# Leaving out the spare TensorE products that fill its waits in a fused two-layer network on one core

## The chip, the cores and the metric

The kernel runs on one core of one Trainium2 chip. The metric is the device time of one execution in microseconds (us); lower is better. A core has TensorE (PE, with its weight loads PEld), VectorE (DVE), ScalarE (ACT), GpSimd (POOL) and SyncE (SP), each working through its own instructions in order and waiting on semaphores for the others.

## What is computed

Two layers are run over x of 4 batches x 512 tokens x 256 features, in float32. Cut to what matters:

```python
x = x + attn(layernorm(x))      # q, k, v by one product; softmax over one score per head
x = x + ffn2(layernorm(x))      # top-1 of 2 experts, FF = 1024, silu(g) * u
x = x + ssm(layernorm(x))       # selective scan, state 8: h = dA * h + dBu; y = sum(h * C) + x * D
x = x + moe(layernorm(x))       # top-6 of 64 experts, F = 176, capacity 64, plus a shared expert
```

## The kernel before

The work is cut by batch (b = 0 to 3, 512 tokens, J = 4 tiles of 128) and by stage. A stage name such as `ssm_sum.2.5` is name, batch, part. The string `plan` (L375) lists all stages in one order written out by hand. `run` (L433) walks this list for each engine, and an engine runs its own piece of a stage if it has one. So one list fixes the order on every engine, and a piece that must wait holds up everything behind it on its engine.

The first part works through attention (`attn_*`), routing (`route_*`) and the two-expert layer (`ffn*`) of all batches. The middle interleaves `ffn*`, the scan (`ssm*`) and the gates of the second expert layer (`gates_in`, `gates`, `places`, `rounds`). Behind the list, `run_pairs` (L445) goes through 32 pairs of experts, one after the other, and the sums at the end follow.

The stages that the prediction speaks of:

- `attn_in` is a layer norm on DVE; `attn_turn` (L673) has PE transpose the normed tiles into `turn_ps` and ACT copy them out; `attn_qkv` (L678, product in L684) is the q, k, v product of one tile, and ACT copies it to `xf` (L914); `attn_score`, `attn_add` and `route_gate` are DVE's, with one exponential each on ACT for `attn_score` and `route_gate`.
- `route_slots` needs two tiny PE products (L693, L694), then DVE (from L1173) works out the rows, and POOL scatters the tokens to memory. `ffn_in` loads them back and transposes them. `ffn` (L705, products in L712) and `ffn_h` (transposes of DVE's result, L652) follow.
- `gates_in` is a norm on DVE (L1101 its last part) with PE transposes (L652) and ACT copies; `gates` is a PE product of 16 records (L780) and DVE's softmax (from L1338); `places` is DVE's top-6 (to L1375), a PE transpose and an ACT copy; `rounds` is DVE's repeated maximum (L1387); `tables` is DVE's (L1415 to L1428, the last two after a PE transpose and an ACT copy), and POOL's gathers of token rows start when it is done.
- `shared_mm` (L794), `shared` (DVE, L1255 and L1260) and `shared_out` (PE, L812) are the shared expert. The first pair of experts starts with `turn_rows(0)` (PE transposes of the gathered rows, L832), then PE waits for `gu_used` (DVE has used the last `shared_mm` product, L874), then comes `gate_up1(0)` (L841).

`awake` (L665) is PE's alone. It multiplies the identity with zeros, twice, 256 columns wide, into `ssm_ps`. Nothing reads that result; the next real product into this bank starts it anew. In batch 0 it waits for POOL's constants, in batch 3 for ACT's last copy out of `ssm_ps`. The list holds 39 of these stages: 16 for batch 0 ahead of and among the attention stages, 23 for batch 3 between `ssm_out.3` and the end of the list.

Each float32 product shows in the trace as two records, so one `awake` stage is four records.

Of the kernel before, what the change touches and what calls it, by code (L numbers as in the profile page):

```python
# [119 lines left out]
def build(nc, x, wq_t, bq, wkv_t, bkv, gate0, wg0_t, wu0_t, wd0_t, wx_t, wdt_t, b_dt, a_log, d_par,  # L120
          gate1_t, wgu1, wd1, shg_t, shu_t, shd_t, out):
    with ExitStack() as ctx:
# [132 lines left out]
        def carve(n):  # L255
# [125 lines left out]
            route_slots.1 ffn.0.0 ffn.0.1 ffn_h.0.0 attn_score.2 awake.0.15 ffn.0.2 ffn_h.0.1 ffn.0.3 attn_turn.3
            attn_add.2 attn_qkv.3.0 ffn_load.1 attn_qkv.3.1 ffn_down.0.0 route_gate.2 ffn_h.0.2 ffn.0.4 ffn_h.0.3
            ffn.0.5 attn_qkv.3.2 attn_qkv.3.3 route_slots.2 ffn_down.0.1 attn_score.3 ffn_h.0.4 attn_add.3 ffn.0.6
            ffn_h.0.5 ffn.0.7 ffn_down.0.2 ffn_h.0.6 route_gate.3 ffn.0.8 ffn_h.0.7 route_slots.3 ffn.0.9
            ffn_down.0.3 ffn_h.0.8 ffn_h.0.9 ffn_down.0.4 ffn_out.0 ffn_in.1 ffn.1.0 ssm_norm.0 ffn.1.1 ffn_h.1.0
            ffn.1.2 ssm_in.0 ssm_proj.0 ffn_h.1.1 ssm_exp.0 ssm_delta.0 ffn.1.3 ffn_down.1.0 ssm.0.0 ffn_h.1.2
            ssm_a.0.0 ffn.1.4 ffn_h.1.3 ffn.1.5 ffn_down.1.1 ssm.0.1 ssm_a.0.1 ssm_sum.0.0 ffn_h.1.4 ssm_a.0.2
            ssm_a.0.3 ssm_a.0.4 ssm.0.2 ffn.1.6 ffn_h.1.5 ssm_sum.0.1 ffn.1.7 ffn_down.1.2 ssm_a.0.5 ssm_sum.0.2
            ssm.0.3 ssm.0.4 ssm.0.5 ssm_a.0.6 ffn_h.1.6 move_sum.0.0 ffn.1.8 ffn_h.1.7 ssm_a.0.7 ffn_load.2 ffn.1.9
# [1126 lines left out]
```

## Time and profile before

| | |
|---|---|
| median of 3 runs | 695.05 us (693.71 to 695.93) |
| the profiled execution: its own time | 695.07 us |
| its span, first to last instruction | 693.3 us |
| mean granted TensorE clock | 0.934 of full |
| busy: PE, DVE, ACT, POOL | 589.8, 514.0, 192.2, 106.4 us |

Times in the trace are us from the span's start. "Granted clock" is the TensorE clock that the throttle allowed in a stretch, as a share of 2.4 GHz; it is at one of two levels, 1.00 (2.4 GHz) or 0.50 (1.2 GHz), and a value between them is a stretch that had both. Releasers in brackets name what ended an engine's idle time. The records of back-to-back PE products overlap by some tenths of a us in the timeline; the chain shows them end to end.

### The profile page before, as it was taken

Reading aid. Unit: us, or ns where it says so; the run is one execution under the profiler, and the core shown is the slowest. Engines: PE = TensorE matmul, PEld = TensorE weight load, DVE = VectorE, ACT = ScalarE, POOL = GpSimd, SP = SyncE. Lnnn points to the kernel's source line nnn. Section 1 sums busy time; section 2 is a strip of 40 time slices with the busy share of each in tenths; the row PEclk is TensorE's granted clock in tenths of the full one; section 3 lists DMA queues with packets and bytes.
Section 4 is the critical chain, followed back from the end, with each engine's and each line's share of the span. In section 5 each row is a group of like instructions: output and inputs, shape, how many; then the busy total and the mean of one; then the engine's idle time right before and its main releaser. Section 6 shows DMA issues by size and latency. Waiting matters only on the chain.

```text
span 693.3 us, 7285 instructions
## 1 busy us (share of the span) xinstructions
PE 589.8 (85%) x2297; PEld 334.7 (48%) x2297; DVE 514.0 (74%) x1126; ACT 192.2 (28%) x375; POOL 106.4 (15%) x120
## 2 busy tenths in 40 slices
PE   7569999789998859987889958949599799999865
PEld 6444565435555346543455513534287344444454
DVE  7989888068895859999689996899978355555355
ACT  1112231136432344322543305413110223323000
POOL 2022020300002000020000030000000456664200
PEclk9889999899999959999799977979899999999999
DMA  7960000419102291010750014993071299996497
GB/s 278 405 208 25 16 32 0 134 66 352 43 0 69 93 353 51 23 38 1 282 182 24 1 38 154 348 333 129 0 251 38 77 330 367 373 374 240 178 413 296
DMA packets 50036, 114.62 MB, mean 165 GB/s; under 512 B 6096, under 2 KB 32464, under 8 KB 49488
## 3 DMA queue, kind: packets, MB, share of 16 engines
q1 hardware_dynamic: 42064, 94.36, 38.0%
q0 software_dynamic: 5632, 17.70, 7.3%
q10 hardware_dynamic: 2304, 2.10, 0.9%
q8 instruction: 20, 0.33, 0.2%
q14 instruction: 16, 0.13, 0.1%
HBM read 83.99 MB, written 30.15 MB: 165 GB/s over the span
## 4 chain that ended last, share of the span: by engine, by line
PE 50%; DVE 33%; DMA 6%; issue 4%; ACT 3%; SPq 2%; POOL 1%; DVEq 0%; POOLq 0%; ACTq 0%
PE gate_ps L712 7%; DVE scan_area L1315 7%; PE gate_ps L841 6%; PE up_ps L712 6%; PE misc_ps L729 5%; DMA bc<-part_rows 4%; DVE scan_area L1311 3%; DVE scan_area L1318 3%; PE turn_ps L652 3%; PE ssm_ps L671 3%; PE ssm_ps L761 3%; PE ssm_ps L859 3%; PE misc_ps L812 3%; PE misc_ps L859 3%; SPq L563 2%
## 5 line engine op out<-in xcount | busy, mean ns | idle before, releaser
L1315 DVE TENSOR_TENSOR_SCAN scan_area<-scan_area 128x1024 f32<-128x1024 f32 x32 | 73.3, 2292 | 4.4 <-ACT scan_area L999 0.9
L712 PE MATMUL gate_ps<-big,front_area 128*128 x144 | 74.8, 645 | 1.4 <-ACT front_area L899 1.4
L761 PE MATMUL ssm_ps<-scan_area,ident 128*128 128x512 f32 x128 | 63.5, 629 | 12.6 <-DVE scan_area L1318 11.9
L712 PE MATMUL up_ps<-big,front_area 128*128 x144 | 70.1, 610 | 0.0
L729 PE MATMUL misc_ps<-big,front_area 128*128 x288 | 65.6, 381 | 4.2 <-ACT front_area L899 3.8
L729 PEld LDWEIGHTS misc_ps<-big,front_area 128*128 128x128 f32 x288 | 54.3, 190 | 18.3 <-issue 11.7
L935 ACT ACTIVATE sig<-gate_ps 128x512 f32<-128x512 f32 (+1 forms) x48 | 28.5, 595 | 105.2 <-PE up_ps L712 65.9
L671 PE MATMUL ssm_ps<-zeros,ident 128*128 128x256 f32 x156 | 42.1, 427 | 15.9 <-ACT front_area L899 12.9
L999 ACT ACTIVATE scan_area<-scan_area,a_col 128x511 f32<-128x511 f32 x64 | 42.2, 714 | 39.8 <-DVE scan_area L1315 35.8
L610 POOL DMA_INDIRECT front_area<-ysorted_dram,slot_idx x16 | 18.5, 1155 | 188.0 <-DMA ysorted_dram<-front_area 184.4
L712 PEld LDWEIGHTS up_ps<-big,front_area 128*128 128x128 f32 x144 | 29.0, 201 | 37.9 <-issue 37.9
L761 PEld LDWEIGHTS ssm_ps<-scan_area,ident 128*128 128x128 f32 x128 | 24.5, 197 | 44.1 <-issue 25.4
L671 PEld LDWEIGHTS ssm_ps<-zeros,ident 128*128 128x128 f32 x156 | 33.1, 217 | 22.8 <-ACT front_area L899 13.6
L1318 DVE TENSOR_TENSOR scan_area<-scan_area,bc 128x1024 f32<-128x1024 f32 x32 | 39.2, 1225 | 1.1
L1255 DVE SCALAR_TENSOR_TENSOR sig<-sig,gate_ps 128x512 f32<-128x512 f32 (+1 forms) x48 | 32.8, 683 | 9.7 <-ACT sig L935 9.3
L1311 DVE TENSOR_TENSOR scan_area<-scan_area,bc 128x1024 f32<-128x1024 f32 x32 | 39.1, 1223 | 0.5
L899 ACT COPY front_area<-turn_ps 128x512 f32<-128x512 f32 (+1 forms) x56 | 31.1, 575 | 25.2 <-PE turn_ps L652 24.2
L712 PEld LDWEIGHTS gate_ps<-big,front_area 128*128 128x128 f32 x144 | 26.8, 204 | 23.2 <-issue 23.2
L635 POOL DMA_INDIRECT part_rows<-bc,att_s x32 | 31.2, 974 | 37.6 <-DVE bc L1446 36.8
L619 POOL DMA_INDIRECT bc<-table,att_s x32 | 30.9, 965 | 28.8 <-DVE att_s L1428 19.4
L652 PE MATMUL turn_ps<-ident,front_area 128*128 128x128 f32 x188 | 29.2, 288 | 6.3 <-DMA front_area<-sorted_dram 4.1
L652 PEld LDWEIGHTS turn_ps<-ident,front_area 128*128 128x128 f32 x188 | 23.6, 148 | 21.7 <-issue 11.9
(236 smaller groups left out, 904.9 us busy)
## 6 DMA issues: line engine op xcount, KB each, us to landing
bc<-bc_dram SPq DMA_DIRECT2D x4, 4096.0 KB, 13.3
part_rows<-zeros SPq DMA_DIRECT2D x16, 768.0 KB, 15.8
big<-in_wgu SPq DMA_DIRECT2D x15, 704.0 KB
front_area<-in_wgu SPq DMA_DIRECT2D x9, 704.0 KB
big<-part_rows SPq DMA_DIRECT2D x8, 768.0 KB, 9.6
...
```

The costliest lines, as they stand in the source:

```text
L652: mm = pe.transpose(turn_ps[slot][0:width, col:col + rows], src, ident[0:rows, 0:rows])
L671: pe.matmul(ssm_ps[:, 0:D], ident[:], zeros[:, 0:D], start=True, stop=True)
L712: mm = pe.matmul(bank[:], xs_t[:, k, j, :], gu0[:, expert_of[b, j], k, g, half * 512:(half + 1) * 512], start=(k == 0), stop=(k == K - 1))
L729: mm = pe.matmul(misc_ps[:, 0:D], h0_t[:, half, c * P:(c + 1) * P], dn0[:, expert_of[b, j], half * 4 + c, :], start=(half == 0 and c == 0) ...
L761: mm = pe.matmul(ssm_ps[:], ident[:], hs[:, g % HS_RING, n, :], start=False, stop=(g % PER_CHUNK == PER_CHUNK - 1 and n == GROUP - 1))
L841: mm = pe.matmul(gate_ps[p % 2][e * CAP:(e + 1) * CAP, 0:FSH], xg_t[:, p % 2, k, e * CAP:(e + 1) * CAP], gu1[p % RING][:, e * K + k, :], s ...
L859: mm = pe.matmul(y_ps[par][e * CAP:(e + 1) * CAP, 0:D], h1_t[0:rows, par, c, e * CAP:(e + 1) * CAP], dn1[p % RING][c][:, e * D:(e + 1) * D ...
L999: nc.scalar.activation(d_a[:, g % 2, n, 1:L], delta[:, c, 1:L], ACT.Exp, scale=a_col[:, c, n0 + n:n0 + n + 1]).then_inc(da_ready, 1)
L1255: stt(out=s, in0=s, scalar=1.0, in1=gate_ps[slot][0:rows, :], op0=ALU.add, op1=ALU.mult).then_inc(silu_steps, 1)
L1311: tt(buf, sp_z[:, c, :].unsqueeze(1).broadcast_to([P, GROUP, L]), bc[:, n0:n0 + GROUP, :], ALU.mult).then_inc(dbu_ready, 1)
L1315: nc.vector.tensor_tensor_scan(buf.rearrange(flat), d_a[:, g % 2, :, :].rearrange(flat), buf.rearrange(flat), 0.0, ALU.mult, ALU.add).then ...
L1318: tt(buf, buf, bc[:, NS + n0:NS + n0 + GROUP, :], ALU.mult).then_inc(hc_ready, 1)
```

## The change

All 39 `awake` stages are taken out of the list. The function `awake` stays, unused, and all other stages keep their order. Cut to its core:

```diff
-            awake.0.0 awake.0.1 awake.0.2 awake.0.3 awake.0.4 awake.0.5 attn_in.0 attn_turn.0 awake.0.6 awake.0.7
-            attn_in.1 attn_qkv.0.0 attn_qkv.0.1 attn_qkv.0.2 attn_in.2 attn_qkv.0.3 awake.0.8 attn_score.0
...
+            attn_in.0 attn_turn.0 attn_in.1 attn_qkv.0.0 attn_qkv.0.1 attn_qkv.0.2 attn_in.2 attn_qkv.0.3
+            attn_score.0 attn_turn.1 attn_add.0 route_gate.0 attn_qkv.1.0 ffn_load.0 attn_qkv.1.1 attn_qkv.1.2
...
```

Only PE's instructions change; those of the other engines are the same, with the same waits. The text of the change is four lines shorter, so a line of before from L641 on has a number lower by 4 after.

PE at the start, before, from just behind `attn_qkv.0.3` to `attn_qkv.2.1` (`front_area` and `scan_area` hold the normed tiles; `ssm_ps<-zeros` are the `awake` products):

```order
L671 MATMUL ssm_ps<-zeros,ident 128x256 x2
L652 MATMUL turn_ps<-ident,scan_area 128x128 x8
L671 MATMUL ssm_ps<-zeros,ident 128x256 x6
L684 MATMUL turn_ps<-w_qkv,front_area 128x288 x2
L671 MATMUL ssm_ps<-zeros,ident 128x256 x4
L684 MATMUL turn_ps<-w_qkv,front_area 128x288 x4
L693 MATMUL misc_ps<-rt,before_me 128x4
L694 MATMUL misc_ps<-rt,ones 128x4
L684 MATMUL turn_ps<-w_qkv,front_area 128x288 x2
L652 MATMUL turn_ps<-ident,scan_area 128x128 x8
L671 MATMUL ssm_ps<-zeros,ident 128x256 x2
L684 MATMUL turn_ps<-w_qkv,front_area 128x288 x4
```

The same place after:

```order
L648 MATMUL turn_ps<-ident,scan_area 128x128 x8
L680 MATMUL turn_ps<-w_qkv,front_area 128x288 x6
L689 MATMUL misc_ps<-rt,before_me 128x4
L690 MATMUL misc_ps<-rt,ones 128x4
L680 MATMUL turn_ps<-w_qkv,front_area 128x288 x2
L648 MATMUL turn_ps<-ident,scan_area 128x128 x8
L680 MATMUL turn_ps<-w_qkv,front_area 128x288 x4
```

The four groups of spare products are gone. The transposes of batch 1 are followed at once by `attn_qkv.1.0` to `attn_qkv.1.2` (two calls each), and those of batch 2 by `attn_qkv.2.0` and `attn_qkv.2.1`.

PE at the end of the list, before, from `ssm_out.3` over `gates_in.3`, `gates.3`, `places.3` and `shared_out.2.1` to `shared_mm.3.0`:

```order
L652 MATMUL turn_ps<-ident,back_t 128x128 x8
L671 MATMUL ssm_ps<-zeros,ident 128x256 x16
L652 MATMUL turn_ps<-ident,xf 128x128 x8
L780 MATMUL misc_ps<-w_g,gate_t 128x64 x8
L671 MATMUL ssm_ps<-zeros,ident 128x256 x16
L652 MATMUL turn_ps<-ident,marked 128x128 x2
L812 MATMUL misc_ps<-w_shd,hsh_t 128x256 x6
L671 MATMUL ssm_ps<-zeros,ident 128x256 x8
L794 MATMUL gate_ps<-gate_t,w_sh 128x512 x2
```

The same place after:

```order
L648 MATMUL turn_ps<-ident,back_t 128x128 x8
L648 MATMUL turn_ps<-ident,xf 128x128 x8
L776 MATMUL misc_ps<-w_g,gate_t 128x64 x8
L648 MATMUL turn_ps<-ident,marked 128x128 x2
L808 MATMUL misc_ps<-w_shd,hsh_t 128x256 x6
L790 MATMUL gate_ps<-gate_t,w_sh 128x512 x2
```

Here 40 spare products in three groups are gone, 16 ahead of `gates_in.3`, 16 ahead of `places.3`, 8 ahead of `shared_mm.3.0`.

PE a little later, before, from the second half of `shared_mm.3.1` over `tables` and `shared_mm.3.2` to the first pair of experts:

```order
L794 MATMUL up_ps<-gate_t,w_sh 128x512 x2
L671 MATMUL ssm_ps<-zeros,ident 128x256 x2
L652 MATMUL turn_ps<-ident,work 128x64
L794 MATMUL gate_ps<-gate_t,w_sh 96x512 x2
L794 MATMUL up_ps<-gate_t,w_sh 96x512 x2
L671 MATMUL ssm_ps<-zeros,ident 128x256 x4
L832 MATMUL turn_ps<-ident,bc 128x128 x2
L841 MATMUL gate_ps<-big,bc 64x352 x4
```

The same place after:

```order
L790 MATMUL up_ps<-gate_t,w_sh 128x512 x2
L648 MATMUL turn_ps<-ident,work 128x64
L790 MATMUL gate_ps<-gate_t,w_sh 96x512 x2
L790 MATMUL up_ps<-gate_t,w_sh 96x512 x2
L828 MATMUL turn_ps<-ident,bc 128x128 x2
L837 MATMUL gate_ps<-big,bc 64x352 x4
```

Two spare products ahead of the transpose of `tables` and four ahead of `turn_rows(0)` (L832) are gone.

## Rows read from the trace of the kernel before

**Rows 1.** The page: engines, chain by engine, the group of the spare products.

```profile
PE 589.8 (85%) x2297; PEld 334.7 (48%) x2297; DVE 514.0 (74%) x1126; ACT 192.2 (28%) x375; POOL 106.4 (15%) x120
...
PE 50%; DVE 33%; DMA 6%; issue 4%; ACT 3%; SPq 2%; POOL 1%; DVEq 0%; POOLq 0%; ACTq 0%
...
L671 PE MATMUL ssm_ps<-zeros,ident 128*128 128x256 f32 x156 | 42.1, 427 | 15.9 <-ACT front_area L899 12.9
```

**Rows 2.** Chain that ended last, 500 to 562 us: start, length, what.

```profile
507.38 6.91 PE ssm_ps L671 x32
...
517.99 6.96 PE ssm_ps L671 x32
...
527.77 3.46 PE ssm_ps L671 x16
...
538.09 0.86 PE ssm_ps L671 x4
...
543.13 1.73 PE ssm_ps L671 x8
...
545.63 1.40 PE gate_ps L841 x8
```

**Rows 3.** DVE's timeline, 512 to 546 us: start, length, what.

```profile
513.23 1.38 DVE L1101 TENSOR_SCALAR xf<-x_res,ln_mv,ln_w 128x256 f32<-128x256 f32 x4
518.03 0.42 DVE L1338 TENSOR_REDUCE sc_s<-misc_ps 128x4 f32<-128x256 f32 x1 [3.42 <-PE misc_ps L780]
...
523.75 0.43 DVE L1375 TENSOR_TENSOR marked<-att_s,sc 128x256 f32<-128x256 f32 x1
...
537.27 0.35 DVE L1419 SCALAR_TENSOR_TENSOR work<-work 64x64 f32<-64x64 f32 x2
...
544.51 0.75 DVE L1260 SCALAR_TENSOR_TENSOR hsh_t<-sig,up_ps 96x256 f32<-96x256 f32 x2
```

**Rows 4.** DVE's timeline, 39 to 66 us.

```profile
39.62 0.17 DVE L1173 COPY rt<-misc_ps 128x8 f32<-128x8 f32 x1 [1.54 <-PE misc_ps L694]
...
41.17 1.36 DVE L1119 TENSOR_TENSOR xf<-xf,b_qkv 128x1152 f32<-128x1152 f32 x1 [0.32 <-ACTq L917]
...
64.36 0.69 DVE L1260 SCALAR_TENSOR_TENSOR front_area<-sig,up_ps 128x512 f32<-128x512 f32 x1
```

**Rows 5.** PE's timeline, 27 to 67 us.

```profile
27.54 5.22 PE L671 MATMUL ssm_ps<-zeros,ident 128*128 128x256 f32 x12 [7.19 <-ACT front_area L899]
...
38.01 1.24 PE L684 MATMUL turn_ps<-w_qkv,front_area 128*128 128x288 f32 x4 [1.58 <-ACT xf L914]
...
48.73 4.05 PE L684 MATMUL turn_ps<-w_qkv,front_area 128*128 128x288 f32 x8
53.17 1.09 PE L652 MATMUL turn_ps<-ident,front_area 128*128 128x128 f32 x8 [0.40 <-DMA front_area<-sorted_dram]
...
63.05 1.88 PE L712 MATMUL up_ps<-big,front_area 128*128 x4
...
65.60 1.03 PE L671 MATMUL ssm_ps<-zeros,ident 128*128 128x256 f32 x4
```

**Rows 6.** Busy time by stretch: PE, PEld, DVE, ACT, POOL; then granted clock, DMA.

```profile
24.00:27.00 3.00, 0.00 (x0) 0.00 (x0) 2.54 (x6) 0.73 (x3) 0.00 (x0) 0.76 1.03 411
30.00:33.00 3.00, 3.00 (x10) 2.39 (x9) 2.75 (x14) 0.00 (x0) 0.00 (x0) 0.61 1.02 406
...
460.00:463.00 3.00, 3.00 (x9) 2.41 (x9) 2.97 (x2) 1.10 (x2) 0.00 (x0) 0.59 1.04 335
```

**Rows 7.** PE's timeline: the gate stages and shared_out of batches 0, 2 and 3.

```profile
241.48 1.97 PE L652 MATMUL turn_ps<-ident,xf 128*128 128x128 f32 x8
244.12 3.68 PE L780 MATMUL misc_ps<-w_g,gate_t 128*128 128x64 f32 x16 [0.68 <-ACT gate_t L899]
...
458.94 4.49 PE L812 MATMUL misc_ps<-w_shd,hsh_t 128*128 128x256 f32 x12
...
516.00 2.00 PE L780 MATMUL misc_ps<-w_g,gate_t 128*128 128x64 f32 x16 [0.67 <-ACT gate_t L899]
```

More of the change, by code:

```diff
@@ L381, in build @@
[L381 to L389, printed above, removed]
-            ssm_sum.0.3 ssm_sum.0.4 ffn_down.1.3 ssm_sum.0.5 ffn_h.1.8 ffn_h.1.9 ssm.0.6 ffn_down.1.4 ssm.0.7
@@ L411, in build @@
-            awake.3.21 awake.3.22 awake.3.23 gates_in.3 gates.3 awake.3.24 awake.3.25 awake.3.26 awake.3.27
-            awake.3.28 awake.3.29 awake.3.30 awake.3.31 places.3 rounds.3.0 rounds.3.1 shared_out.2.1 awake.3.32
-            awake.3.33 rounds.3.2 awake.3.34 awake.3.35 shared_mm.3.0 shared_mm.3.1 awake.3.36 shared.3.0 tables.3
-            shared.3.1 shared.3.2 shared_mm.3.2 awake.3.37 awake.3.38"""
+            attn_in.0 attn_turn.0 attn_in.1 attn_qkv.0.0 attn_qkv.0.1 attn_qkv.0.2 attn_in.2 attn_qkv.0.3
@@ new lines, in build @@
+            ffn_down.1.2 ssm_a.0.5 ssm_sum.0.2 ssm.0.3 ssm.0.4 ssm.0.5 ssm_a.0.6 ffn_h.1.6 move_sum.0.0 ffn.1.8
+            ffn_h.1.7 ssm_a.0.7 ffn_load.2 ffn.1.9 ssm_sum.0.3 ssm_sum.0.4 ffn_down.1.3 ssm_sum.0.5 ffn_h.1.8
+            ffn_h.1.9 ssm.0.6 ffn_down.1.4 ssm.0.7 ffn_out.1 ffn_in.2 ssm_sum.0.6 ssm_sum.0.7 ffn_load.3 move_sum.0.1
+            ssm_out.0 ffn.2.0 ssm_norm.1 ffn.2.1 ffn_h.2.0 ffn.2.2 ssm_in.1 ssm_proj.1 gates_in.0 gates.0 ssm_exp.1
+            places.0 ffn_h.2.1 ssm_delta.1 ssm_a.1.0 rounds.0.0 ffn.2.3 ssm.1.0 ffn_down.2.0 ffn_h.2.2 ffn.2.4
@@ new lines, in build @@
+            move_sum.2.1 shared.0.0 ssm_sum.2.7 ssm_out.2 ssm_norm.3 shared_mm.0.2 shared.0.1 ssm_in.3 ssm_proj.3
+            gates_in.2 shared.0.2 shared_out.0.0 ssm_exp.3 weights_ahead.3 ssm_delta.3 shared_out.0.1 shared_mm.1.0
+            shared.1.0 ssm.3.0 ssm_a.3.0 ssm_a.3.1 shared_mm.1.1 shared.1.1 shared.1.2 shared_mm.1.2 ssm_a.3.2
+            gates.2 places.2 ssm_a.3.3 ssm_a.3.4 ssm.3.1 shared_out.1.0 rounds.2.0 weights_more.3 ssm.3.2
+            shared_out.1.1 ssm_sum.3.0 ssm.3.3 shared_mm.2.0 shared_mm.2.1 shared.2.0 ssm.3.4 shared.2.1 ssm_sum.3.1
@@ L416, in stage_of @@
+            ssm_a.3.5 ssm_a.3.6 shared_mm.2.2 ssm_sum.3.2 ssm_sum.3.3 ssm_sum.3.4 ssm.3.5 shared.2.2 move_sum.3.0
+            ssm_sum.3.5 ssm_sum.3.6 ssm_a.3.7 ssm.3.6 ssm_sum.3.7 ssm.3.7 rounds.2.1 rounds.2.2 shared_out.2.0
+            move_sum.3.1 ssm_out.3 gates_in.3 gates.3 places.3 rounds.3.0 rounds.3.1 shared_out.2.1 rounds.3.2
+            shared_mm.3.0 shared_mm.3.1 shared.3.0 tables.3 shared.3.1 shared.3.2 shared_mm.3.2"""
         def stage_of(name, batch, part="0"):
```

42 lines of the change are left out of this document (19 added, 23 removed).

## The prediction

> **What bounds the kernel now.** I read the page first, for the shares. The trap is in its first line: PE is busy 85% of the span, and the spare products alone are 42.1 us of that [rows 1]. The chain of waits says something else. It runs over PE for half of the span and over DVE for a third [rows 1], so the two take turns, and a product that PE does while DVE sets the pace costs nothing. Then the chain in order of time, at the end of the list: the spare products stand on it as 6.91, 6.96, 3.46, 0.86 and 1.73 us, together 18.9 us [rows 2]. They stand there because each runs up to the moment at which the next real stage can start, or a little past it. What would have been waited for without them must be read from DVE's timeline [rows 3, 4]. Last the granted clock by stretch, and products of one shape at both clocks [rows 5 to 7], since a product that nobody reads can still have an effect on the next one.
>
> What these show of the clock: PE had nothing to do for 7.19 us before 27.54 [rows 5], and in that time the granted clock fell (0.76 in 24 to 27, where it did nothing at all) [rows 6]. The spare products that followed began at 1.2 GHz: 12 records took 5.22 us [rows 5], where 32 take 6.91 at the full clock [rows 2]. In 30 to 33 the mean is 0.61, so 2.3 of these 3 us were still at 1.2 GHz and the clock came back at about 32.3, after 4.8 us of steady work. In 460 to 463 the mean is 0.59 [rows 6]: back at about 462.5, 3.5 us after the group that began at 458.94 [rows 7]. A product at 1.2 GHz takes 1.6 to 1.85 times as long: the gate stage 3.68 us against 2.00 [rows 7], eight records of the q, k, v product 4.05, so 2.02 for four, against 1.24 [rows 5].
>
> **The start (16 stages).** Up to 27 us DVE goes from norm to norm and PE is ahead of it; I cost the first nine stages at nothing. The cover is that DVE takes up the first scores only after its third norm, when PE and ACT have long had the operand ready; were it gone, each product there would be late by its own price at the lower clock.
>
> Then, after ACT's copies at 27.5, qkv.1.0 and qkv.1.1 run at once, at 1.2 GHz, 2.02 us each, and end at 31.6. In place of spare products PE has nothing until 38.01, when ACT frees a buffer [rows 5]. That is 6.4 us, close to the 7.19 that let the clock fall. So qkv.1.2 starts at 38.01 as before but at 1.2 GHz: +0.8. The two tiny products of the routing add 0 to 0.5 (no row at the lower clock; I take 0.25). DVE is waiting for them: 1.54 us at 39.62 [rows 4], so the routing of batch 0 is 1.05 late, and with it POOL's scatter and the load for ffn_in.0. qkv.1.3 adds another 0.8, and DVE waits for it at 41.17 (0.32 now) [rows 4]: DVE is 1.9 late from there. The spare stage ahead of qkv.2.0 goes, four records at the lower clock (5.22 / 12 x 4 = 1.7); the operand of qkv.2.0 is now 1.9 later, so it starts at 48.7 to 48.9, all but the same, and at 1.2 GHz as before (4.05 for eight records) [rows 5].
>
> The two lines meet at the first expert products. PE's (ffn.0.1) ended at 63.05 + 1.88 = 64.93 and now ends at 66.0. DVE's result (64.36 + 0.69 = 65.05 [rows 4]) comes at 66.95, and PE's transposes wait for that. Behind them stood one more spare stage, 0.87 us from start to start (65.60 [rows 5] to the next product). PE goes on 1.9 - 0.87 = **1.0 us late**, and here PE is busy without gaps, so this stays.
>
> What is open is when the clock comes back. PE's steady work now begins at 48.7 and stops at 52.8 to wait for the load of ffn_in.0, until about 53.17 + 1.05 = 54.2 [rows 5]. That is 4.1 us of work, between the two recoveries read above (3.5 and 4.8). If the clock is back, nothing more is lost. If not, the transposes and q, k, v products that follow cost about 2.7 more (1.8 for eight records of q, k, v by the two prices above, 0.9 for ten transposes at nearly twice their time), of which 1.0 is hidden, since DVE's result is 1.0 behind PE's. So the start costs 1.0 to 2.7; I take **1.5**, nearer to the low end, because a clock that comes back by 56 costs nothing extra.
>
> **The end of the list (23 stages).** Before, PE filled the 6.9 us until gates_in.3. Now it has nothing from 507.4 until DVE's first two normed tiles, at 513.23 + half of 1.38 = 513.9 [rows 3]. 6.5 us idle: the clock falls, as above. The transposes and gate products at the lower clock are those of batch 0: 241.48 to 244.12 + 3.68 = 247.80, so 6.3 us [rows 7], and end at 520.2 against 516.00 + 2.00 = 518.0 [rows 7]. That is **+2.2**. DVE waits for them (3.42 us already [rows 3]), so it all counts.
>
> DVE's gates and places take 6.15 us either way, to 523.75 + 0.43 = 524.18 before [rows 3] and 526.4 now. Before, the third group of spare products kept PE until 517.99 + 6.96 = 524.95 [rows 2]: 0.8 given back. The transpose at the lower clock costs 0.3 more. DVE's maxima start later by 2.2 - 0.8 + 0.3: **+1.7**.
>
> DVE has the slots for tables at 537.27 + 0.35 = 537.6 [rows 3], but PE is in shared_mm and spare products until 538.09 + 0.86 = 538.95 [rows 2]. Now DVE is ready at 539.3. Is PE? Its shared_out.2.1 starts at 527.0 and takes 4.5 as in batch 2 [rows 7], to 531.5. Without the next spare products (3.46 [rows 2]) shared_mm.3.0 and 3.1 follow, 6.9 us, to 538.4. It is free 0.9 us ahead of DVE. So tables is late by 539.3 - 538.95 = 0.35, and another 1.35 us are given back. shared_mm.3.2 starts with it and DVE is done with it at 544.51 + 0.75 = 545.26 [rows 3], now 545.6. The first pair began at 545.63 behind the last spare products (to 544.86) [rows 2]; its rows had landed by then, and their gathers are 0.35 late too. It begins at 545.9 to 546.1: the end of the list costs **0.3 to 0.5**. I take 0.3. From there PE's steady loop over 32 pairs is the same.
>
> Between the two places nothing changes but by the shift: each cold spell there falls somewhat otherwise, either way.
>
> **Sum.** The profiled execution took 695.07, 1.8 more than its span, and is the same as the median, 695.05. 695.07 + 1.5 + 0.3 = **696.9**. With the ends 1.0 to 2.7 and 0.3 to 0.5, and half a us for each of the shifted cold spells' sides, this forecast's own range is 695.4 to 698.8.
>
> The Trainium skill ("TensorE: Matmul & The Clock Gate", HAM oscillation) prices this another way: what a throttled stretch costs is its length times one half. For single products the trace agrees (3.68 against 2.00). Applied to every added throttled stretch, about 18 us at the end and 10 at the start by my working, it would give an estimate of 14 us and 709; here most of such a stretch is waiting for DVE, which no clock shortens.
>
> **Rivals.**
>
> *The clock stays up.* Then only what the spare products delayed is left: 0.87 at 65.6, and at the end 0.2 of waiting at 514, 0.8 at 524.95 and 1.35 before tables, which DVE's chain hands on in full. 695.07 - 0.9 - 2.3 = 691.9. It needs 6.4 us without work at the full clock; 7.19 us [rows 5] did not pass without a fall. Decided at 514. 8%.
>
> *All is hidden.* DVE's lateness of 1.9 meets the 0.87 given back and some wait behind it that I did not see, and the end comes out at zero: 695.1. For it: the chain changes engine often. Against: both lines are late by 1.0 at 66 us and the stretch behind has no gap. 12%.
>
> *The clock comes back late,* slower. The place is 54 to 62 us: if the clock stays at 1.2 GHz through the first expert products, 7.8 us of PE's time hold half of the work, 3.9 lost, 1.0 of it hidden by DVE: start 3.9. At the end the same length from 527.0 brings shared_mm.3.1 to 540.4, 1.1 behind DVE's slots: end 1.2 to 1.4. 700.2. It decides from the point at which the clock is not back by 56 us. For it: the work is broken by a wait at 52.8 to 54.2. Against: both recoveries above. 18%.
>
> *The change takes effect as waits and nothing else* (the chain's 18.9 us vanish, 676): nothing in DVE's timeline gets shorter with it. Under 1%.
>
> **The numbers.** Forecast 62%, the rivals 8, 12 and 18%. A change of under 0.3% (2.1 us) can't be told from none here. The forecast's range is cut by 697.15 a little above its middle: 35% same, 27% slower. Same: 35 and 12, 47%; slower: 27 and 17, 44%; faster 9%. The range 693.8 to 700.3 leaves out the fast rival and the worst of the slow one.
>
> **What would show it.** The granted clock at 0.50 from 33 or 36 to beyond 42, and around 514 to 530. The q, k, v record group at 38 at about 2.0 us. DVE's wait before the first exponential of batch 1 (L1119 before) about 2.2 us. The gate products at the end at 3.7, DVE's maxima 1.7 later than the shift from the start; tables' transpose with no PE work ahead of it. If the first pair starts more than 3 us late against 545.63, the start or the recovery was mis-sized; if it starts earlier, the clock did not fall.

## The result, and the profile after

| | before | after |
|---|---|---|
| median, in turn on one chip | 694.98 us (691.05 to 696.43, 20 runs) | 697.87 us (695.15 to 702.68, 20 runs) |
| the profiled execution, its span | 695.07, 693.3 us | 696.94, 695.2 us |
| mean granted TensorE clock | 0.934 | 0.909 |

The ratio is 1.0047, 95% interval 1.0029 to 1.0064: the kernel without spare products is slower, by 2.0 to 4.4 us, about 3.3. Each ratio here and below is worked out from all the single executions of both kernels, so it need not be the quotient of the two medians (1.0042 here). The prediction had 696.9 as the time, +1.9 us. The profiled execution of after happens to show just that; that is luck, and the median shows more.

The page of after, engines and chain by engine; they answer to [rows 1]:

```profile
PE 562.8 (81%) x2141; PEld 310.7 (45%) x2141; DVE 513.8 (74%) x1126; ACT 192.7 (28%) x375; POOL 105.2 (15%) x120
...
PE 42%; DVE 39%; DMA 7%; issue 4%; ACT 4%; SPq 2%; POOL 1%; DVEq 0%; POOLq 0%; ACTq 0%
```

PE lost 156 instructions and 42.1 us of spare work, but its busy time fell by only 27.0 us: the other 15 are real products that now take longer. The chain has 8 points less of PE and 6 points more of DVE: what stood there as spare products stands there now as waiting for DVE.

Busy time by stretch, after; columns as in [rows 6], the granted clock is the third number from the end:

```profile
24.00:27.00 3.00, 0.00 (x0) 0.00 (x0) 2.54 (x6) 0.62 (x2) 0.00 (x0) 0.50 1.02 411
...
36.00:39.00 3.00, 0.88 (x2) 0.74 (x3) 1.86 (x12) 0.79 (x3) 0.00 (x0) 0.50 1.08 312
39.00:42.00 3.00, 3.00 (x9) 2.31 (x9) 0.80 (x6) 0.40 (x1) 0.00 (x0) 0.50 1.06 332
...
51.00:54.00 3.00, 2.13 (x5) 1.07 (x4) 2.86 (x11) 0.80 (x2) 0.00 (x0) 0.70 0.66 207
54.00:57.00 3.00, 2.17 (x13) 1.59 (x14) 2.69 (x12) 1.45 (x3) 0.00 (x0) 1.00 0.00 0
...
514.00:534.00 20.00, 9.61 (x35) 8.36 (x36) 11.47 (x49) 1.96 (x4) 0.40 (x1) 0.50 0.46 156
534.00:536.00 2.00, 2.00 (x8) 1.30 (x7) 1.90 (x6) 0.00 (x0) 0.00 (x0) 0.98 0.00 0
```

The clock is at its low level from 36 to 42, back before 54, and at the low level for all 20 us from 514 to 534, where before had the full clock (1.00, its row stands in experiment 3). That is the forecast's picture.

PE's timeline at the start, after; it answers to [rows 5]:

```profile
38.12 2.29 PE L680 MATMUL turn_ps<-w_qkv,front_area 128*128 128x288 f32 x4 [6.26 <-ACT xf L910]
40.20 0.43 PE L689 MATMUL misc_ps<-rt,before_me 128*128 128x4 f32 x2
...
56.36 2.21 PE L680 MATMUL turn_ps<-w_qkv,front_area 128*128 128x288 f32 x8 [0.46 <-ACT front_area L895]
...
67.35 0.66 PE L648 MATMUL turn_ps<-ident,front_area 128*128 128x128 f32 x4 [1.22 <-DVE front_area L1256]
67.84 1.45 PE L708 MATMUL gate_ps<-big,front_area 128*128 x3
```

The third tile of batch 1 starts at 38.12 as before and takes until 40.20, at 1.2 GHz. By 56.36 the clock is up: eight records take 2.21 us. PE then waits 1.22 us for DVE at 67.35, and `ffn.0.2` starts at 67.84 against 66.47.

DVE's timeline at both ends, after; it answers to [rows 3, 4]:

```profile
41.10 0.17 DVE L1169 COPY rt<-misc_ps 128x8 f32<-128x8 f32 x1 [2.90 <-PE misc_ps L690]
...
43.45 1.36 DVE L1115 TENSOR_TENSOR xf<-xf,b_qkv 128x1152 f32<-128x1152 f32 x1 [1.12 <-ACTq L913]
...
516.55 1.38 DVE L1097 TENSOR_SCALAR xf<-x_res,ln_mv,ln_w 128x256 f32<-128x256 f32 x4
...
523.72 0.42 DVE L1334 TENSOR_REDUCE sc_s<-misc_ps 128x4 f32<-128x256 f32 x1 [5.78 <-PE misc_ps L776]
...
531.18 0.49 DVE L1383 MAX8 keep<-work 128x8 f32<-128x320 f32 x1 [1.33 <-ACT work L895]
...
542.77 0.35 DVE L1415 SCALAR_TENSOR_TENSOR work<-work 64x64 f32<-64x64 f32 x2
...
548.81 0.75 DVE L1256 SCALAR_TENSOR_TENSOR hsh_t<-sig,up_ps 96x256 f32<-96x256 f32 x2
```

Against [rows 4], DVE has the routing's sums 1.48 us late (41.10) and starts on the second batch's q, k, v 2.28 late (43.45). The last norm is 3.32 late (516.55 against 513.23 in [rows 3]), the softmax behind it 5.69, the slots for `tables` (L1415, L1419 before) 5.50, the last `shared` 4.30. So from the norm on the end adds 2.4 at the softmax, 2.2 at the slots and 1.0 at the last `shared`.

PE's timeline at the end, after; it answers to [rows 2, 7]:

```profile
517.39 1.94 PE L648 MATMUL turn_ps<-ident,xf 128*128 128x128 f32 x8 [6.66 <-DVE xf L1097]
520.01 3.67 PE L776 MATMUL misc_ps<-w_g,gate_t 128*128 128x64 f32 x16 [0.68 <-ACT gate_t L895]
530.00 0.66 PE L648 MATMUL turn_ps<-ident,marked 128*128 128x128 f32 x2 [6.33 <-DVE marked L1371]
...
543.18 0.28 PE L648 MATMUL turn_ps<-ident,work 64*128 64x64 f32 x1 [1.31 <-DVE work L1415]
...
549.61 1.40 PE L837 MATMUL gate_ps<-big,bc 128*64 128x352 f32 x8 [1.54 <-DVE hsh_t L1256]
```

PE waits for DVE in front of each step but the gate products, which wait 0.68 for ACT's copy and take 3.67. The first pair starts at 549.61, 3.98 late, of which 3.32 came with the last norm: the end costs 0.66 here. Of the 3.32, `ffn.0.2` had only 1.37; the rest came in the long stretch between, in which no stage was changed. Yet the whole span is only 1.9 longer. Of the other 2.1, 1.8 are in a place that the prediction took for the same in both: in before, PE stops once more at the third pair (below, experiment 9).

### The profile page after: what moved, and what is told of

It is laid out like the page before. It is cut to its first block, busy times and chain, and to the rows that moved or that the text cites. A ratio compares the mean times of both kernels' runs of the same rounds, so it can differ in the third digit from the quotient of the medians.

```text
span 695.2 us, 6972 instructions
## 1 busy us (share of the span) xinstructions
PE 562.8 (81%) x2141; PEld 310.7 (45%) x2141; DVE 513.8 (74%) x1126; ACT 192.7 (28%) x375; POOL 105.2 (15%) x120
## 4 chain that ended last, share of the span: by engine, by line
PE 42%; DVE 39%; DMA 7%; issue 4%; ACT 4%; SPq 2%; POOL 1%; DVEq 0%; POOLq 0%; ACTq 0%
DVE scan_area L1311 7%; PE gate_ps L837 6%; PE gate_ps L708 6%; PE up_ps L708 5%; PE misc_ps L725 4%; DMA bc<-part_rows 4%; DVE scan_area L1307 3%; DVE scan_area L1314 3%; PE turn_ps L648 3%; PE ssm_ps L855 3%; PE misc_ps L855 3%; DVE work L1385 2%; DVE sig L1251 2%; DVE keep L1383 2%; PE misc_ps L808 2%
## 5 line engine op out<-in xcount | busy, mean ns | idle before, releaser
L708 PE MATMUL gate_ps<-big,front_area 128*128 x144 | 72.7, 630 | 1.4 <-ACT front_area L895 1.4
L995 ACT ACTIVATE scan_area<-scan_area,a_col 128x511 f32<-128x511 f32 x64 | 42.3, 714 | 41.0 <-DVE scan_area L1311 36.2
L648 PE MATMUL turn_ps<-ident,front_area 128*128 128x128 f32 x188 | 30.6, 297 | 20.2 <-DVE front_area L1097 8.9
L680 PE MATMUL turn_ps<-w_qkv,front_area 128*128 128x288 f32 x64 | 25.0, 551 | 22.1 <-ACT front_area L895 15.9
L611 POOL COPY xf<-sc 128x256 f32<-128x256 f32 x4 | 2.1, 527 | 190.9 <-DVE sc L1343 190.9
## 6 DMA issues: line engine op xcount, KB each, us to landing
front_area<-in_wgu SPq DMA_DIRECT2D x9, 704.0 KB, 14.6
```

The costliest lines, as they stand in the source:

```text
L648: mm = pe.transpose(turn_ps[slot][0:width, col:col + rows], src, ident[0:rows, 0:rows])
L708: mm = pe.matmul(bank[:], xs_t[:, k, j, :], gu0[:, expert_of[b, j], k, g, half * 512:(half + 1) * 512], start=(k == 0), stop=(k == K - 1))
L995: nc.scalar.activation(d_a[:, g % 2, n, 1:L], delta[:, c, 1:L], ACT.Exp, scale=a_col[:, c, n0 + n:n0 + n + 1]).then_inc(da_ready, 1)
```

## The experiments

The theory: the spare products act through the clock alone, and the start makes most of the loss. Its rivals: what they earn lies at the end (the gate products at 3.67 instead of 2.00); or it isn't the clock at all, but the order and the number of the instructions. Where an expectation has theories with letters, these are its own. All kernels are cut from the kernel before; each median and ratio is against executions of before on the same chip in the same session (12 of the kernel, or 10, and 33 to 35 of before). Before's own median was 695.1 to 697.7 from chip to chip, so the ratio counts. The diffs are cut to the stages that change.

**Experiment 1: only the 16 stages of batch 0 out.**

```diff
-            awake.0.0 awake.0.1 awake.0.2 awake.0.3 awake.0.4 awake.0.5 attn_in.0 attn_turn.0 awake.0.6 awake.0.7
...
-            route_slots.1 ffn.0.0 ffn.0.1 ffn_h.0.0 attn_score.2 awake.0.15 ffn.0.2 ffn_h.0.1 ffn.0.3 attn_turn.3
```

> Only the 16 spare stages of batch 0 are out. If the loss comes from the lower clock at the start, as predicted: +1.0 to +1.9 us against before (about 0.2%), DVE's wait for the second q, k, v copy 2 us longer, the first expert products behind ffn_h.0.0 1.0 to 1.4 us late. If the loss is made at the end of the list: 0 here. If removing the stages is neutral there and only moves code, 0.

Measured: 698.28 against 695.5 us, ratio 1.0043 (1.0024 to 1.0062), 3.0 us slower, where 1.0 to 1.9 was expected. The start alone costs as much as the whole change. In its profile the clock comes back late at the products that the prediction had left open (PE's timeline; eight records that take 2.21 us in the first profile of after):

```profile
57.06 3.90 PE L683 MATMUL turn_ps<-w_qkv,front_area 128*128 128x288 f32 x8 [0.46 <-ACT front_area L898]
```

**Experiment 2: only the 23 stages of batch 3 out.**

```diff
-            shared_out.2.0 move_sum.3.1 ssm_out.3 awake.3.16 awake.3.17 awake.3.18 awake.3.19 awake.3.20 awake.3.21
...
-            shared.3.1 shared.3.2 shared_mm.3.2 awake.3.37 awake.3.38"""
+            shared.3.1 shared.3.2 shared_mm.3.2"""
```

> Only the 23 spare stages of batch 3 are out. The theory of the prediction: the gate products at the end start at 1.2 GHz, +2.2 at DVE's softmax, of which 0.3 to 0.7 are left at the first pair of experts; time +0.3 to +1.0 us. Rival: the end makes most of the measured 3.3 us, +2 us or more, because more of the 2.2 us stays than I counted. The two runs together should give the whole, 3.3 us, if the places are independent.

Measured: 693.65 against 695.5 us, ratio 0.997 (0.9955 to 0.9986): 2.1 us faster. Leaving out the products at the end is a gain, where I had put +0.3. So they earn nothing at the end, taken as a whole, as far as this run goes; experiment 8 finds no gain in leaving them out. Its profile is the forecast's for the end, with the clock low behind it (PE's timeline, this kernel):

```profile
513.21 1.94 PE L650 MATMUL turn_ps<-ident,xf 128*128 128x128 f32 x8 [8.08 <-DVE xf L1099]
515.82 3.68 PE L778 MATMUL misc_ps<-w_g,gate_t 128*128 128x64 f32 x16 [0.68 <-ACT gate_t L897]
...
539.57 3.56 PE L792 MATMUL gate_ps<-gate_t,w_sh 128*96 128x512 f32 x4 [0.30 <-ACT bc L897]
```

**Experiment 3: all 39 stages stay, each product 8 columns wide.** Same instructions in the same places with the same waits, and little for PE to do in them.

```diff
-                    pe.matmul(ssm_ps[:, 0:D], ident[:], zeros[:, 0:D], start=True, stop=True)
+                    pe.matmul(ssm_ps[:, 0:8], ident[:], zeros[:, 0:8], start=True, stop=True)
```

> All 39 spare stages stay in their places with their waits, but each product is 8 columns wide instead of 256, so PE has the same number of instructions and little work. If what counts is the clock that the work keeps up, the time is that of the changed kernel, +2.5 to +3.5 us, with the clock at 1.2 GHz at 38 and at 516. If what counts is anything that hangs on the instructions being there (their place in the code, PE being awake to its semaphores), the time is that of before, within 1 us.

Measured: 698.71 against 695.5 us, ratio 1.0044 (1.0023 to 1.0064). Busy time by stretch, this kernel:

```profile
27.00:45.00 18.00, 14.93 (x48) 11.66 (x48) 12.63 (x48) 2.38 (x7) 1.38 (x2) 0.52 0.90 320
514.00:534.00 20.00, 17.18 (x76) 16.08 (x76) 11.30 (x44) 1.96 (x4) 0.40 (x1) 0.54 0.32 110
```

and before:

```profile
27.00:45.00 18.00, 12.61 (x48) 9.71 (x48) 15.00 (x49) 2.07 (x6) 2.78 (x2) 0.85 0.91 326
514.00:534.00 20.00, 19.33 (x95) 15.66 (x94) 13.74 (x47) 1.96 (x4) 0.40 (x1) 1.00 0.26 91
```

The records show PE busy for 14.93 of 18 us, and the granted clock is at its low level nearly all the time (0.52; before had 0.85 there). With every instruction and wait in place the loss is the full one. So it isn't the order or the count of instructions but the work that the products give the engine.

**Experiment 4: six of the 39 out,** those that reach past the moment at which real work could start: the one ahead of `ffn.0.2`, the last of the second group at the end, and the last four of the list.

```diff
-attn_score.2 awake.0.15 ffn.0.2
+attn_score.2 ffn.0.2
...
-awake.3.28 awake.3.29 awake.3.30 awake.3.31 places.3
+awake.3.28 awake.3.29 awake.3.30 places.3
...
-awake.3.34 awake.3.35 shared_mm.3.0 shared_mm.3.1 awake.3.36 shared.3.0
+awake.3.34 shared_mm.3.0 shared_mm.3.1 shared.3.0
...
-shared.3.1 shared.3.2 shared_mm.3.2 awake.3.37 awake.3.38"""
+shared.3.1 shared.3.2 shared_mm.3.2"""
```

> 33 of 39 spare stages stay; out are those that the chain shows to delay the next real stage: the one before ffn.0.2, the last one before the transpose of places.3, the last one before shared_mm.3.0 and the one before tables, and the two before the first pair. If waiting for DVE is what the others fill, and the clock stays up without these six: -0.9 at 66 us and -2.1 at the first pair, together -3.0 us against before (0.996). Rival: the clock falls in a gap left by them, or what is given back is lost behind another wait: -1 us or less.

Measured: 694.1 (688.04 to 695.72) against 695.5 us, ratio 0.9966 (0.9943 to 0.9989), 2.4 us faster, near the 3.0 expected; with 0.8 to 4.0 as its interval it all but rules out the rival's 1 or less.

**Experiment 5: the changed kernel again,** with a second profile.

> The changed kernel once more, beside the next three on one chip. The start alone measured +3.0 us and the end alone -2.1 us, which adds up to +0.9, against +3.3 for the whole. If the two parts are independent and the gap is noise: about +1 to +2 us now. If what the end gives is lost when the start is out as well: +3 us again.

Measured: 697.87 against 695.08 us, ratio 1.0046 (1.0022 to 1.0071): the same as the first time. The profile is not the same. PE's timeline at the start, this execution:

```profile
54.30 2.48 PE L648 MATMUL turn_ps<-ident,front_area 128*128 128x128 f32 x10 [0.80 <-DMA front_area<-sorted_dram]
57.25 4.21 PE L680 MATMUL turn_ps<-w_qkv,front_area 128*128 128x288 f32 x8 [0.46 <-ACT front_area L895]
...
69.04 1.88 PE L708 MATMUL gate_ps<-big,front_area 128*128 x4
```

The eight records that took 2.21 us at 56.36 in the first profile take 4.21 here, and `ffn.0.2` starts at 69.04, 2.6 late instead of 1.4. The clock comes back late. The time is the expectation's second case: what the end gives by itself (-2.1) doesn't show when the start is out as well.

**Experiments 6 and 7: only the first nine stages out (`awake.0.0` to `0.8`), and only the next five (`0.9` to `0.13`).**

```diff
-            awake.0.0 awake.0.1 awake.0.2 awake.0.3 awake.0.4 awake.0.5 attn_in.0 attn_turn.0 awake.0.6 awake.0.7
-            attn_in.1 attn_qkv.0.0 attn_qkv.0.1 attn_qkv.0.2 attn_in.2 attn_qkv.0.3 awake.0.8 attn_score.0
+            attn_in.0 attn_turn.0
+            attn_in.1 attn_qkv.0.0 attn_qkv.0.1 attn_qkv.0.2 attn_in.2 attn_qkv.0.3 attn_score.0
```

```diff
-            attn_turn.1 attn_add.0 awake.0.9 awake.0.10 route_gate.0 awake.0.11 attn_qkv.1.0 awake.0.12 ffn_load.0
-            awake.0.13 attn_qkv.1.1 attn_qkv.1.2
+            attn_turn.1 attn_add.0 route_gate.0 attn_qkv.1.0 ffn_load.0
+            attn_qkv.1.1 attn_qkv.1.2
```

> Only awake.0.0 to awake.0.8 are out, those ahead of and among the first batch's attention, up to 19 us. Prediction: 0 (DVE sets the pace there and PE's results have over 2 us in hand, also at 1.2 GHz). Rival: part of the start's 3.0 us comes from here, +1 us or more, because the clock is down when the work at 27 us begins.

> Only awake.0.9 to awake.0.13 are out, the five between 27.5 and 36 us (ten products). If they carry the start's loss by keeping the clock up for attn_qkv.1.2, the routing products and attn_qkv.1.3: DVE 2.0 to 2.7 us late at attn_score.1, and with the stage before ffn.0.2 still there, nothing of it is given back: +2.5 to +3.0 us. Rival: the loss is spread over the sixteen, +1 us or less here.

Measured: 696.48 against 695.08, ratio 1.0026 (1.0001 to 1.005), and 696.82, ratio 1.0029 (1.0011 to 1.0047). The five cost 2.0 us (0.8 to 3.3): less than the 2.5 to 3.0 of the clock theory, more than the rival's 1, and no sharp test between them. The nine cost 1.8, with an interval that all but reaches zero; I had put them at nothing, and the rival had +1 or more. PE's timeline with the nine out:

```profile
8.82 1.94 PE L652 MATMUL turn_ps<-ident,front_area 128*128 128x128 f32 x8 [8.82 <-DVE front_area L1101]
11.44 6.50 PE L684 MATMUL turn_ps<-w_qkv,front_area 128*128 128x288 f32 x16 [0.68 <-ACT front_area L899]
...
57.33 3.81 PE L684 MATMUL turn_ps<-w_qkv,front_area 128*128 128x288 f32 x8 [0.46 <-ACT front_area L899]
```

The first transposes and q, k, v products run in part at 1.2 GHz, which DVE hides for the most part: in this profile the first group behind batch 0's attention starts at 28.25 instead of 27.54 [rows 5], 0.7 us late, and so do the routing's sums (40.34 against 39.62 in [rows 4]). But the clock falls elsewhere too, and eight records at 57.33 take 3.81 us: `ffn.0.2` is 3.1 late. Why that happens here, some 40 us behind the last stage taken out, isn't settled by one execution.

**Experiment 8: the 23 stages at the end and the one ahead of `ffn.0.2` out.**

```diff
-attn_score.2 awake.0.15 ffn.0.2
+attn_score.2 ffn.0.2
...
-            shared.3.1 shared.3.2 shared_mm.3.2 awake.3.37 awake.3.38"""
+            shared.3.1 shared.3.2 shared_mm.3.2"""
```

> Out are the 23 stages of batch 3 and awake.0.15, the one before ffn.0.2; the 15 at the start that come before it stay. Sum of what was measured and read: -2.1 us for the end, -0.9 for the one stage, together -3.0 us against before. Rival: the end's gain was chance or the stage is hidden: -1.5 us or less.

Measured: 694.12 against 695.08 us, ratio 1.0001 (0.9975 to 1.0026). Expected was -3.0; what came is the rival's case, -1.5 or less. It should have been no slower than experiment 2 and is not told from before. The two intervals (0.9955 to 0.9986, 0.9975 to 1.0026) overlap only just, so the gain of experiment 2 isn't confirmed by this one.

**Experiment 9: before again,** as if it were a change.

> The kernel before, unchanged, taken as if it were a change. It says what a comparison of this kind gives when nothing differs, and gives a second profile of before. Theory A (the fall of the clock in before's last part is chance from one execution to the next): the ratio is 1.000 within 0.002, and the 34.2 us from the last norm tile to the first pair's tanh product, seen in the first profile of before, may as well be 37.5 here, with spare products at half clock between 518 and 526 and rounds.3 late. Theory B (the 34.2 us belongs to the kernel with all 39 spare stages, and the 37.5 to those with fewer): 34.2 again. Also: the 2.1 us in which PE issued nothing after the first pair should not be here again.

Measured: ratio 0.9995 (0.9972 to 1.0017). The comparison finds nothing where nothing is. The second profile of before is another picture than the first. Its PE timeline at the end, and its clock:

```profile
504.36 7.07 PE L671 MATMUL ssm_ps<-zeros,ident 128*128 128x256 f32 x32
512.61 1.26 PE L652 MATMUL turn_ps<-ident,xf 128*128 128x128 f32 x8 [1.18 <-issue]
514.54 3.08 PE L780 MATMUL misc_ps<-w_g,gate_t 128*128 128x64 f32 x16 [0.68 <-ACT gate_t L899]
517.41 9.42 PE L671 MATMUL ssm_ps<-zeros,ident 128*128 128x256 f32 x32
526.67 0.38 PE L652 MATMUL turn_ps<-ident,marked 128*128 128x128 f32 x2
...
553.91 1.40 PE L841 MATMUL gate_ps<-big,bc 128*64 128x352 f32 x8 [2.08 <-issue]
```

```profile
517.00:520.00 3.00, 3.00 (x9) 2.54 (x10) 1.76 (x5) 0.42 (x1) 0.00 (x0) 0.50 0.00 0
520.00:523.00 3.00, 3.00 (x11) 2.43 (x9) 2.75 (x18) 0.00 (x0) 0.40 (x1) 0.66 0.50 177
```

The clock falls during the gate products although 7.07 us of spare work stand ahead of them, and then the second group of spare products itself runs at 1.2 GHz: 9.42 us instead of 6.96 [rows 2]. DVE's places were done at 523.80. The real transpose can't start until 526.67, because PE works in order and its queue is full of products that nobody reads. DVE's maxima (L1387) start 15.80 us behind the last norm (511.77), where the first profile of before has 525.69 - 513.23 = 12.46, and after has 14.63. DVE's timeline, this execution:

```profile
523.38 0.42 DVE L1375 TENSOR_TENSOR marked<-att_s,sc 128x256 f32<-128x256 f32 x1
...
527.57 0.49 DVE L1387 MAX8 keep<-work 128x8 f32<-128x320 f32 x1 [3.77 <-ACT work L899]
```

and the first of before:

```profile
525.69 0.49 DVE L1387 MAX8 keep<-work 128x8 f32<-128x320 f32 x1 [1.51 <-ACT work L899]
```

The Trainium skill ("TensorE: Matmul & The Clock Gate", on the HAM clock gate) says that the count of slow products at the start of one and the same kernel differs from run to run. The two profiles of before agree, and show it in the kernel's last part too (6.96 against 9.42 us for the same 32 records).

The wait of 2.08 us at the third pair was there again, which I had expected not to be. In the first profile of before it is this row:

```profile
552.06 1.40 PE L841 MATMUL gate_ps<-big,bc 128*64 128x352 f32 x8 [2.11 <-issue]
```

PE needs two things there: DVE's result of the second pair, which needs ACT's tanh, and ACT's copy of the third pair's turned rows (L1033), which stands behind that tanh in ACT's order. ACT's timeline, the second execution:

```profile
552.03 0.32 ACT L1044 ACTIVATE bc<-gate_ps 128x176 f32<-128x176 f32 x1 [2.33 <-PE gate_ps L841]
553.44 0.37 ACT L1033 COPY bc<-turn_ps 128x256 f32<-128x256 f32 x1 [1.09 <-remote]
```

The products for the tanh start at 549.84 and take 1.40, so they are done at 551.24, and ACT takes them up 0.8 later; in the first profile of before it is 1.5 (550.87 against 549.36). The copy comes another 1.09 later here, and PE starts 0.1 behind its end in both (553.91 against 553.81, 552.06 against 551.96): it is ACT's copy that PE waits for last. From the first to the last of the pairs' tanh products on DVE both executions of before have 95.8 us; the eight of after (twice) and experiments 1, 2, 4, 6, 7 and 8 have 94.0. What holds ACT up isn't shown. It isn't the stages at the end by themselves, since 1, 6 and 7 keep them all. Nor is it a rule of the number of stages: experiment 3 has all 39 and no such stop (its 95.75 us come from a low clock at the first pairs, as the 96.12 of experiment 12), and experiment 11 with 30 stages has one of 2.27 us. So 1.8 us of before's length lie in this loop in both its profiles, and whether the change takes them away or chance does stays open.

**Experiments 10 and 11: the end taken apart.** In both the stage ahead of `ffn.0.2` is out. Experiment 10 keeps of the end only the first group (`awake.3.16` to `3.23`, ahead of `gates_in.3`); experiment 11 keeps all but that group.

```diff
-awake.3.24 awake.3.25 awake.3.26 awake.3.27 awake.3.28 awake.3.29 awake.3.30 awake.3.31 places.3
+places.3
```

```diff
-ssm_out.3 awake.3.16 awake.3.17 awake.3.18 awake.3.19 awake.3.20 awake.3.21 awake.3.22 awake.3.23 gates_in.3
+ssm_out.3 gates_in.3
```

> Of the end only the first group of eight spare stages stays, the one ahead of gates_in.3; all later ones and the one ahead of ffn.0.2 are out. Theory A (at the end, what costs is that spare products stand in the way of real ones, and what they earn is the gate products of gates.3 at the full clock, 2.2 us): the gate products run at 2.0, DVE's softmax is not late, nothing stands ahead of the placed tokens' transpose and of tables, and the time is the least of all: about 1 us below the kernel without any end stage, 692 to 693.5, ratio 0.994 to 0.997. Theory B (the first group alone can't hold the clock through the idle time after it, and DVE's chain decides the rest): as without end stages, 693.5 to 694.5, ratio 0.997 to 0.999. Slower than before would speak against both.

> The opposite: the first group of eight ahead of gates_in.3 and the one stage ahead of ffn.0.2 are out, the other 15 end stages stay. Theory A: the gate products run at 1.2 GHz, 3.7 us, so DVE's softmax is 2.2 late; the spare products behind them begin at 1.2 GHz too and run past the moment at which the placed tokens could be transposed, which adds 1 to 3 us; no gain from the clock left. Worse than before: 696 to 699, ratio 1.002 to 1.006. Theory B (the later groups are harmless, since DVE has slack there): 693.5 to 695, as without end stages.

Measured: experiment 10, 692.96 (689.47 to 696.34) against 697.65 us, ratio **0.9934** (0.9906 to 0.9963), 4.6 us faster than before, Theory A's time or a little better. Experiment 11, 698.77, ratio 1.0008 (0.9986 to 1.0029), between its two theories. PE's timeline of experiment 10:

```profile
513.92 3.22 PE L779 MATMUL misc_ps<-w_g,gate_t 128*128 128x64 f32 x16 [0.68 <-ACT gate_t L898]
523.48 0.66 PE L651 MATMUL turn_ps<-ident,marked 128*128 128x128 f32 x2 [6.33 <-DVE marked L1374]
...
536.65 0.27 PE L651 MATMUL turn_ps<-ident,work 64*128 64x64 f32 x1 [1.03 <-DVE work L1418]
```

and of experiment 11:

```profile
513.51 3.68 PE L780 MATMUL misc_ps<-w_g,gate_t 128*128 128x64 f32 x16 [0.68 <-ACT gate_t L899]
516.98 8.69 PE L671 MATMUL ssm_ps<-zeros,ident 128*128 128x256 f32 x32
525.50 0.38 PE L652 MATMUL turn_ps<-ident,marked 128*128 128x128 f32 x2
```

In 10, PE is idle when DVE comes with the places: the transpose follows at once, and the maxima start 13.51 us behind the norm. In 11 it has to get through 8.69 us first, and they start at 16.35. By the two ratios the difference is 0.74%, 5 us, of which the profiles show 2.84 at the maxima and 4.34 at the first pair (33.74 and 38.08 us behind the norm).

Experiment 8 is the common base of the two: 10 has the first group more than 8 (0.9934 against 1.0001, the intervals apart, on two chips), 11 the 15 later stages more (1.0008 against 1.0001, the same). So the first group is worth having, and the later ones alone show no gain. But it isn't worth it in the way that Theory A had: in the profile of 10 the gate products take 3.22 us, not 2.0, and DVE's softmax comes 1.2 us later behind the norm than in the first profile of before (6.03 against 4.80). That is still less than the 3.67 in the profile of 8, and part of the gain lies further on: `shared_mm.3.2`'s first products take 1.96 us in 10 and 3.56 in 8 and 2.

In the times of experiment 10 the luck of the clock can be seen as well: its four slowest executions (695.4 to 696.3 us) have a mean granted clock of 0.914 to 0.916, the other eight (689.5 to 693.5) 0.928 to 0.933.

**Experiment 12: experiment 4 again.**

> The kernel with 33 spare stages again (out: the one ahead of ffn.0.2, the last of the second end group, and the last four of the list). The first time it stood at 0.9966 of before, with executions of 688.0 to 695.7. Theory A (shorter groups end before the real work can start, so they cost nothing, and the clock's gain stays): again 0.995 to 0.998, with some executions near 688. Theory B (the first result was the luck of that chip): 0.999 to 1.001.

Measured: 695.03 against 697.65 us, ratio 0.9957 (0.9932 to 0.9982). It held, 0.9966 and 0.9957, though no execution came near 688 (the lowest is 691.79). Its profile has 8.56 us for the shorter second group (28 records, at the lower clock), where the first had 6.26: so it too reached past DVE's places when the clock fell. Its interval overlaps that of experiment 10; which of the two is better isn't settled.

Where the 14 profiled executions stood, in us, each read from a row's start (PE L712's third group; DVE L1101, L1387, L1453, with the lines of before):

| kernel | `ffn.0.2` starts | last norm tile | norm to maxima | norm to first tanh product | first to last of these |
|---|---|---|---|---|---|
| before | 66.47 | 513.23 | 12.46 | 34.19 | 95.83 |
| 9, before again | 66.56 | 511.77 | 15.80 | 37.54 | 95.79 |
| after | 67.84 | 516.55 | 14.63 | 34.86 | 93.99 |
| 5, after again | 69.04 | 515.27 | 14.64 | 36.55 | 94.00 |
| 1, start out | 68.54 | 514.81 | 15.79 | 37.52 | 94.01 |
| 6, nine out | 69.59 | 517.53 | 12.46 | 34.19 | 94.00 |
| 7, five out | 69.55 | 514.74 | 15.80 | 37.53 | 94.00 |
| 3, narrow | 68.65 | 515.31 | 14.89 | 36.36 | 95.75 |
| 2, end out | 66.83 | 512.37 | 14.64 | 36.55 | 93.99 |
| 8, end and one out | 67.41 | 512.76 | 14.63 | 36.55 | 93.99 |
| 4, trimmed | 65.74 | 509.25 | 12.66 | 32.88 | 93.99 |
| 12, trimmed again | 67.34 | 513.71 | 14.93 | 35.60 | 96.12 |
| 10, first group kept | 66.16 | 511.15 | 13.51 | 33.74 | 94.67 |
| 11, later groups kept | 65.58 | 510.05 | 16.35 | 38.08 | 99.08 |

The columns from the norm on say it for the end. With all its spare products in place (before, 9, 1, 6, 7) it is 12.5 or 15.8 us long to the maxima, by the luck of the clock: the gate products take 2.00 us in the two short ones and 3.02 to 3.19 in the three long ones. Without them (after, 5, 2, 8) it is 14.6 each time. To the first tanh product the two sorts are alike in the mean, 36.2 and 36.1 us.

The first two columns hold something else: from `ffn.0.2` to the last norm, where no kernel differs from another, it takes 443.5 (experiment 4) to 448.7 us (after), and in before alone 446.8 and 445.2. A single profile can be off by more than the whole effect there.

## Why the prediction was right, and where it wasn't

The mechanism held, in each of its steps: PE's idle time lets the clock fall, DVE waits for the slow products, and the loss is a few us, since most of a slow stretch is waiting that no clock shortens. 697.9 is within the forecast's own range, 695.4 to 698.8. But the chances leaned a little to "within 0.3%" (47 to 44), and it is slower by 0.47%: the terms were too small on balance, and some of them had the wrong place.

- **The start, +1.5 (1.0 to 2.7): too small.** By experiment 1 the whole start costs 3.0 us (1.7 to 4.3). The step that failed was "a clock that comes back by 56 costs nothing extra", taken as the likelier case. In the first profile of after it came back in time, and `ffn.0.2` was 1.4 late. In the second, and in that of experiments 1 and 6, it didn't: 4.21, 3.9 and 3.81 us for eight records that take 2.21. Over the three executions with all 16 stages out (after twice, 1) `ffn.0.2` is 1.3 to 2.5 late, 2.0 in the mean against the two of before (68.5 and 66.5). In experiments 6 and 7 it is 3.1 and 3.0 late, in part since there the 0.87 of the stage ahead of it isn't given back. That was the mechanism of my rival "the clock comes back late", and its condition, low through the first expert products, was asking too much: low through the q, k, v products at 57 is enough. The other step is "between the two places nothing changes but by the shift": at the last norm the three stand 3.1 late in the mean (515.5 against 512.5 for before, 9 and 2), about 1 more than at `ffn.0.2`. With a spread there of 1.5 us in before alone, whether this 1 belongs to the change is open.
- **The size of its steps.** I priced `qkv.1.2` at +0.8, as 2.02 - 1.24; but 1.24 is the time from its first record's start to its last one's end, and what counts is when the next product can start: 38.12 to 40.20 in after is 2.08, where before has 38.01 to 39.08, so +1.0. `qkv.1.3` gave the 0.8 that I had for it (40.92 to 42.77 against 39.44 to 40.49), the tiny products 0.4, not 0.25. With the 0.1 by which 38.12 is behind 38.01, DVE's second wait came to 2.28 late, not 1.9.
- **The first nine stages, at nothing:** they cost 1.8 us (0.1 to 3.5) by experiment 6. DVE does hide most of what they do to the first products; the rest is only shown as a total.
- **The end, +0.3 to 0.5.** In the profile of after the steps come out near the forecast: +2.4 at the softmax (2.2), +2.2 at DVE's maxima and slots (1.7), 0.9 at the transpose of `tables` (0.35; 543.18 against 538.95, less 3.32), +0.66 at the first pair. But "+2.2" and "0.8 given back" are both read from before's better execution. In its other one the clock falls in spite of the spare products: the gate products take 3.08 us already, and the second group ends at 526.67, 2.9 behind DVE's places (523.80), so only some of the 2.2 is new and 2.9 are given back. Experiments 1 and 7 show this too (37.5 against 34.2 us to the first pair's product). I read one execution as the kernel. Over all profiles the end costs nothing up to the first pair (36.1 us without, 36.2 with), which is near my 0.3. The times say less than that, and not with one voice: experiment 2 measured -2.1 (-3.1 to -1.0), experiment 8, with one stage more out, +0.1 (-1.7 to +1.8). Where the 2.1 lie isn't shown; in the profile of 2 the stretch from the norm to the first pair is longer than in the first of before (36.55 against 34.19), and the pair loop is 1.8 shorter.
- **The pair loop, "the same":** in the profiles it is 1.8 us shorter, for a reason that isn't shown (experiment 9). The stop was in the trace of before, and I hadn't looked for PE's idle time inside the loop.
- **Sums that don't come out.** The five spare lengths on the chain add up to 19.9 us, not 18.9, so the last rival's time is 675. By the two prices named, eight records of q, k, v cost 1.6 more at the lower clock, not 1.8; measured are 4.21 - 2.21 = 2.0. With half a us on either side the range would begin at 695.9, not 695.4, and no row stands behind that half us: the stretch that it is for differs by 1.5 us between the two profiles of before. None of these changes the verdict.

The sum that the runs give is start +3.0, end -2.1, together +0.9; both at once measured +3.3 (twice). The intervals of these are each 1 to 1.5 us wide to a side, about 2 us for such a gap, so 2.4 is a little more than chance readily gives. Two things may close it. If experiment 8 is taken for the end (+0.1) in place of experiment 2, there is no gap. And the profiles of 1, of 2 and of both out are all without the 1.8 us of the pair loop: if the change takes them away, experiments 1 and 2 count them twice, and the sum of the parts is +2.7. That is worked out, not shown.

The rule of the Trainium skill ("TensorE: Matmul & The Clock Gate", HAM oscillation) prices a throttled stretch at half of its length. Mean clocks of 0.934 and 0.909 are 91.5 and 126.5 us at the low level (twice the missing share of the span), 35 more, and an estimate by that rule of 17.5 us. The runs give 3.3. As I read it, it holds where PE always has a product to do; here PE was idle for half of such a stretch (9.61 busy of 20 us from 514).
